# Short-key attention: paired scores on four 32-row groups, and a new order of work per group of eight units

## The reference, cut to what matters

```python
# layer 0, q = layernorm(x), k = v = ctx (77 rows per batch)
qh, kh, vh = (proj(q, Wq, bq), proj(k, Wk, bk), proj(v, Wv, bv))   # 16 heads of 16
scores = einsum('bhqd,bhkd->bhqk', qh, kh) / sqrt(16)
scores = where(mask[:, None] == 0, -1e9, scores)
attn = softmax(scores, axis=-1)
out = einsum('bhqk,bhkd->bhqd', attn, vh) ... @ Wo.T + bo
x = x + tanh(g_xattn[0]) * out

# layer 2, a = the result of the causal self-attention, no mask
c = relu(attention(a, ctx) @ Wo2 + bo2)
c = layernorm(c + c, g2, b2)
f = relu(c @ Wf + bf)
x = x + tanh(g_xattn[2]) * layernorm(c + f, g3, b3)
```

## Time and profile before

| | |
|---|---|
| median of 3 runs | 2646.04 us (2645.72 to 2651.75) |
| the profiled execution's own time | 2645.53 us |
| its span in the profile | 2643.8 us |
| PE matmul busy | 2394.4 us (91%) |
| PE weight loads busy | 1437.0 us (54%) |
| DVE / ACT / POOL busy | 1609.2 / 1298.3 / 1310.7 us (61 / 49 / 50%) |
| `attend_stage`, first scores to the last update | 29.5 to 252.6 us of the span |
| `cross_stage`, first scores to the last update | 1694.6 to 1970.2 us of the span |

### The profile page before, as it was taken

One profiled execution on the slowest core, in us unless ns is written; L12 is line 12 of the kernel. 1 busy time (PEld: TensorE's weight loads), 2 busy tenths in 40 slices (PEclk: granted clock), 3 DMA queues, 4 the chain that ended last, 5 costly groups with the idle time before them and its releaser, 6 DMA issues. The chain is left out here.

```text
span 2643.8 us, 42280 instructions
## 1 busy us (share of the span) xinstructions
PE 2394.4 (91%) x12771; PEld 1437.0 (54%) x12787; DVE 1609.2 (61%) x3275; ACT 1298.3 (49%) x2567; POOL 1310.7 (50%) x2112
## 2 busy tenths in 40 slices
PE   6997999999996986899999999899969966999997
PEld 3554786666663553345444453455546653666664
DVE  5885674655554976777868767598866653221221
ACT  4664454444442883566666666567644421222221
POOL 3665773234445652233443535467865214656663
PEclk9998999999998997999999999999989987999999
DMA  4001000000100005131231311010013151322222
GB/s 142 6 1 54 15 0 1 1 1 1 48 1 16 1 1 128 38 91 37 62 89 33 101 49 49 25 33 17 1 34 135 49 201 29 48 45 44 48 44 28
DMA packets 86128, 115.34 MB, mean 44 GB/s; under 512 B 15480, under 2 KB 65536, under 8 KB 84272
## 3 DMA queue, kind: packets, MB, share of 16 engines
q1 hardware_dynamic: 67408, 92.65, 11.7%
q0 software_dynamic: 18528, 20.31, 4.8%
HBM read 78.01 MB, written 34.64 MB: 43 GB/s over the span
## 5 line engine op out<-in xcount | busy, mean ns | idle before, releaser
L3458 ACT ACTIVATE L2S_pT<-L2S_t_ps 128x512 f32<-128x512 f32 (+3 forms) x768 | 356.5, 491 | 221.6 <-PE L2S_t_ps L3279 213.0
L3522 DVE TENSOR_REDUCE L2S_mx<-L2S_s_ps 128x1 f32<-128x768 f32 (+7 forms) x384 | 350.2, 951 | 104.7 <-PE L2S_s_ps L3202 104.1
L3279 PE MATMUL L2S_t_ps<-L2S_q,L2S_k 98*128 98x512 bf16 (+3 forms) x768 | 249.6, 335 | 17.4 <-DMA L2S_q<-L2S_mrow 7.3
L3764 POOL TENSOR_SCALAR_AFFINE_SELECT L2S_pT<-L2S_pT 128x128 f32<-128x128 f32 x512 | 151.2, 310 | 174.0 <-ACT L2S_pT L3458 169.9
L3201 PE MATMUL L2S_s_ps<-L2S_k,L2S_q 96*128 96x512 bf16 (+3 forms) x768 | 200.0, 333 | 11.5 <-DVE L2S_mx L3522 7.6
L622 POOL TENSOR_TENSOR L_prob<-L_prob,L_rc 128x616 f32<-128x616 f32 x64 | 82.2, 1285 | 231.2 <-DVE L_rc L555 231.2
L4140 DVE TENSOR_TENSOR L3B_h<-L3B_si,L3B_u_ps 128x512 f32<-128x512 f32 x71 | 48.8, 688 | 237.0 <-PE L3B_u_ps L4083 237.0
L4057 POOL DMA_INDIRECT out<-L3B_y,L3F_rows x71 | 114.7, 1616 | 134.5 <-DVE L3B_y L4146 122.3
L3279 PEld LDWEIGHTS L2S_t_ps<-L2S_q,L2S_k 98*128 98x128 bf16 x768 | 73.0, 98 | 197.8 <-ACT L2S_pT L3458 128.4
L3379 PE MATMUL L2S_o_ps<-L2S_pT,L2S_v 128*32 128x512 f32 (+3 forms) x1536 | 166.7, 507 | 0.0
L319 PE MATMUL L_scores<-weights,L_xT 128*128 128x308 f32 x512 | 143.1, 423 | 2.3 <-ACT L_xT L442 1.6
(11 more groups left out here) (548 smaller groups left out, 5748.1 us busy)
## 6 DMA issues: line engine op xcount, KB each, us to landing
qk_parts<-L2S_part SPq DMA_DIRECT2D x84, 128.0 KB, 2.3
L2S_q<-qk_parts SPq DMA_DIRECT2D x32, 192.0 KB, 3.4
L2S_k<-qk_parts SPq DMA_DIRECT2D x30, 192.0 KB, 3.4
L2S_q<-qk_parts SPq DMA_DIRECT2D x32, 128.0 KB, 3.2
L3F_w<-in_L_gu SPq DMA_DIRECT2D x8, 512.0 KB, 7.5
weights<-in_L_w SPq DMA_DIRECT2D x8, 512.0 KB, 9.7
out<-x_sb SPq DMA_DIRECT2D x8, 512.0 KB, 4.0
expert_rows<-L_xn SPq DMA_DIRECT2D x8, 512.0 KB, 3.3
```

Of the source, the lines that this page charges most:

```text
L3279: nc.tensor.matmul(o[:, lo:512], k6[:, q % 2, j, kt * P:(kt + 1) * P], q6[:, q % 2, c, j, lo:512], start=True, stop=True).then_inc(s["t_fu ...
L3458: nc.scalar.activation(pT[:, st % SLOTS, j, lo:512], t_ps[j % 2][:, lo:512], ACT.Exp, scale=SK).then_inc(s["exp_done"], 1)
L3522: nc.vector.tensor_reduce(dst, src, AX.X, ALU.max).then_inc(s["mx_done"], 1)
L3764: nc.gpsimd.affine_select(out=edge, in_=edge, compare_op=ALU.is_ge, fill=0.0, base=0, pattern=[[1, P]], channel_multiplier=-1).then_inc(s[ ...
```

## The change

In both stages:

- `S_ps` is one tile of four banks. `scores(U)` is called for even `U` only and does two units: for each half of the heads (`hf`) four matmuls of 32 rows x 154 columns (two heads of 16 features, 2 x 77 keys), one for each 32-row group `j`, into bank `j`, columns `hf * 154` on. In `attend_stage` four bf16 mask matmuls of 308 columns come first, one for each bank. It waits for `shifted >= U`: both units of the pair before have been subtracted. The start value 2 of `shifted` is gone. DVE reads a unit as 4 banks x 2 heads x 77 where it was 2 banks x 4 heads x 77.
- The step loops and the table are replaced by an order written out per group, one for each engine. The ring's list is rewritten to match.
- In `cross_stage` `stats` of a group, its `rstd` and tile 0 of `scaled` come one group earlier than before, `update` one group earlier, half of the `x` pieces a group earlier, and the program has `G + 4` group steps where it had `G + 5`.

The diff, cut to its core (ACT's order is cut; the pieces keep their bodies):

```diff
-        S_ps = [ctx.enter_context(nc.psum_tensor(f"L0_scores{i}", [P, 2, 512], F32)) for i in range(2)]
+        S_ps = ctx.enter_context(nc.psum_tensor("L0_scores", [P, ROW_GROUPS, 512], F32))   # ROW_GROUPS, WIDE = 4, 2 * NC
...
             def scores(U):                                      # attend_stage, PE
-                pe.wait_ge(shifted, U + 1)
-                for a in range(2):
-                    nc.tensor.matmul(S_ps[U % 2][:, a, 0:BK], identb[:], wide(maskb[...], [P, 4, NC]), start=True, stop=False)
-                for a in range(2):
-                    mm = nc.tensor.matmul(S_ps[U % 2][:, a, 0:BK], qT[64 * a:64 * a + 64, g % 2, hf, i * P:(i + 1) * P],
-                                          kblk[64 * a:64 * a + 64, b % 2, hf, :, :], start=False, stop=True)
-                mm.then_inc(s_full, 1)
+                if U:
+                    pe.wait_ge(shifted, U)
+                for j in range(ROW_GROUPS):
+                    nc.tensor.matmul(S_ps[:, j, 0:2 * WIDE], identb[:], wide(maskb[...], [P, 4, NC]), start=True, stop=False, skip_group_check=True)
+                for hf in range(2):
+                    for j in range(ROW_GROUPS):
+                        mm = nc.tensor.matmul(S_ps[:, j, hf * WIDE:(hf + 1) * WIDE], qT[32 * j:32 * j + 32, g % 2, hf, i * P:(i + 1) * P],
+                                              kblk[32 * j:32 * j + 32, b % 2, hf, 2 * (j % 2):2 * (j % 2) + 2, :],
+                                              start=False, stop=True, skip_group_check=True)
+                mm.then_inc(s_full, 2)
...
             def unit(U):                                        # both stages, DVE
-                s = S_ps[U % 2][:, :, 0:BK].rearrange("p a (h k) -> p a h k", k=NC)
+                s = S_ps[:, :, U % 2 * WIDE:(U % 2 + 1) * WIDE].rearrange("p j (h k) -> p j h k", k=NC)
...
-            dve.sem_inc(shifted, 2)
...
+            # attend_stage, PE, group n (conditions at the ends left out)
+            scores(8n)     turn(8n-3)  turn_x(n+1,0)  values(odd n)  turn_x(n+1,1)  turn(8n-2)  combine(n-2,3)
+            scores(8n+2)   gather(n-1,0)  turn(8n-1)  query(n+1,0)  turn(8n)
+            scores(8n+4)   gather(n-1,1)  turn(8n+1)  query(n+1,1)  turn(8n+2)
+            scores(8n+6)   combine(n-1,0)  turn(8n+3)  combine(n-1,1)  combine(n-1,2)  turn(8n+4)
+            # attend_stage, DVE
+            unit(8n)    unit(8n+1)                                  total(8n)    total(8n+1)
+            unit(8n+2)  unit(8n+3)  stats(n+3,0)                    total(8n+2)  total(8n+3)
+            unit(8n+4)  unit(8n+5)  blocks (odd n) or masks (even)  total(8n+4)  total(8n+5)
+            unit(8n+6)  unit(8n+7)  stats(n+3,1)                    total(8n+6)  total(8n+7)
+            # attend_stage, POOL: the eight divides, with rstd(n+2) and update(n-2,0..3) between, values (odd n)
+            # cross_stage, PE, group g
+            scores(8g)     turn(8g-4)  forward(g-3,1)  turn(8g-3)  forward(g-3,2)  turn(8g-2)  turn_x(g+1,1)
+            scores(8g+2)   turn(8g-1)  forward(g-3,3)  gather(g-1,0)  gather(g-1,1)
+            scores(8g+4)   turn(8g)  combine(g-1,0)  turn_n(g-2,0)  turn(8g+1)  query(g+1,0)  turn(8g+2)
+            scores(8g+6)   turn_n(g-2,1)  combine(g-1,1)  query(g+1,1)  turn(8g+3)  turn_x(g+2,0)  values(odd g)  forward(g-2,0)
+            # cross_stage, DVE
+            unit(8g)    unit(8g+1)  join(g-3,0)  total(8g)
+            unit(8g+2)  total(8g+1)  unit(8g+3)  total(8g+2)  join(g-3,1)  join(g-3,2)
+            unit(8g+4)  total(8g+3)  unit(8g+5)  join(g-3,3)  total(8g+4)  total(8g+5)
+            unit(8g+6)  stats(g-1,0)  unit(8g+7)  stats(g-1,1)  total(8g+6)  blocks (odd g)  total(8g+7)
+            # cross_stage, POOL: the eight divides, with values, scaled(g-2,1..3), update(g-4,1..3), rstd(1,g-3),
+            # rstd(0,g-1) between, and update(g-3,0), scaled(g-1,0) at the end
```

More of the change, by code:

```diff
@@ L1320, in finish_tail @@
                 mm.then_inc(ring_full, 1)
-            piece = {"x": turn_x, "q": query, "o": gather, "c": combine, "n": turn_n, "f": forward, "v": values, "t": turn_tail, "e": finish_tail}
             turn_x(0, 0)
@@ L1576, in _ @@
+            dve.wait_ge(gain_done, 1)
+            for i in range(CH):
+                update(G - 1, i)
         @block.gpsimd
@@ L1649, in _ @@
             pool.wait_ge(gain_done, 1)
-            for s in range(LAST):
-                g, u = divmod(s, UN)
-                if 0 <= s - 2 < UNITS:
-                    divide(s - 2)
-                if (g, u) in ((0, 5), (0, 6)):
-                    bias_tail(u - 5)
-                if (g, u) == (0, 7):
+            for g in range(SPAN):
+                now, old, older, oldest = g < G, 1 <= g <= G, 2 <= g < HERE + 2, 3 <= g <= G + 2
+                if now:
+                    divide(UN * g)
+                if g == 1:
@@ new lines, in _ @@
+                if older:
+                    scaled(g - 2, 1)
+                if now:
+                    divide(UN * g + 1)
+                if older:
+                    scaled(g - 2, 2)
+                if now:
+                    divide(UN * g + 2)
+                if 4 <= g < G + 3:
+                    update(g - 4, 1)
+                if g == 1:
+                    scale_tail(4, 2, 2, 2)
+                if now:
+                    divide(UN * g + 3)
+                if 4 <= g < G + 3:
+                    update(g - 4, 2)
@@ new lines, in _ @@
+                if oldest:
+                    rstd(1, g - 3)
+                if now:
+                    divide(UN * g + 4)
+                if older:
+                    scaled(g - 2, 3)
+                if g == 0:
+                    bias_tail(0)
+                if now:
+                    divide(UN * g + 5)
+                if 4 <= g < G + 3:
+                    update(g - 4, 3)
+                if g == 0:
+                    bias_tail(1)
+                if g == 1:
+                    scale_tail(6, 2, 3, 3).then_inc(tail_done, 1)
@@ L1682, in pipelined @@
+                if old:
+                    rstd(0, g - 1)
+                if now:
+                    divide(UN * g + 6)
+                    divide(UN * g + 7)
+                if 3 <= g < G + 2:
+                    update(g - 3, 0)
+                if 1 <= g < HERE + 1:
+                    scaled(g - 1, 0)
 def pipelined(eng, phases, n=T, unroll=2, ring=2, order=None):
```

605 lines of the change are left out of this document (409 added, 196 removed).

## The result

The changed kernel takes 2625.76 us (median of 4 runs, 2623.97 to 2627.77), the kernel before 2648.62 on the same chip: ratio 0.9914, 95% interval 0.9897 to 0.9931, so 22.9 us faster. The forecast was 2615 with a range of 2594 to 2640. The profiled execution took 2625.5 us, its span is 2623.8.

The account below looks back on a forecast made before the run. PE was taken to bound most groups of both stages, with DVE and POOL close behind after the change. Savings of 14.9 us in `attend_stage` and 16.3 in `cross_stage`, in all 31.2 off 2645.5, gave 2615 us, range 2594 to 2640.

Parts of the forecast that it names:

- Bound and PE's price: Both stages: PE bounds most groups; a pair of scores costs 0.72 us, 1.35 with masks, 3.3 us less per group.
- The rival that the four row tiles don't overlap: Both stages: PE's row tiles don't run side by side, up to 6.6 us a group against the sum, 2676; chance 0.10.
- DVE's terms: Both stages: DVE's reads of scores stay at 1.52 us a unit; bounds 0 and 0.6 us a group.
- The key blocks: DVE in `attend_stage`: key blocks take 1.8 us in a heavy group (every other group, with the value projection).
- rival C: Both stages: orders fit better than walked, groups at the larger sum; attend -20, cross -24, 2601 or below; chance 0.12.
- Forecast 185.5 for eight groups: `attend_stage`: eight groups fall from 199.9 to 185.5 us, -14.4, with heavy groups at 25 and the last at 20.
- the wait for the pair buffer: PE's scores wait until both units of the pair before are subtracted; expected to stay under 1 us a group.
- `cross_stage`, full groups: `cross_stage` groups 3 to 6: from 121.2 to 112 us, 28.0 each, with PE, DVE and POOL all over 0.9 busy.
- Rival D: Both stages: something else paces them, a divide-to-turn chain or the ring; within 5 us of 2646; chance 0.04.
- `cross_stage`, the first three: `cross_stage` groups 0 to 2: from 76.9 to 24 + 26.5 + 23.5 = 74 us, -2.9.
- the first `scaled`: `cross_stage`: POOL's last piece of a group waits for ACT's next `normalise`, divides behind it; within 28.0 per full group.
- `cross_stage`, ends: `cross_stage`: group 7 goes from 24.7 to 26.5 us (+1.8), the end behind the last divide from 46 to 40.

Follow-up runs that it names:

- e2: Changed kernel with the old unpaired scores in two buffers, so the new order alone; 2635.58 us, ratio 0.9947 to the kernel before.
- e8: Changed kernel without the gain multiplication in POOL's residual update of `cross_stage`; 2616.09 us, ratio 0.9868 to the kernel before.
- e11: Changed kernel with POOL's first `scaled` in `cross_stage` moved behind the next group's first divide; 2617.9 us, ratio 0.9883 to the kernel before.
- e4: Changed kernel with ten unread filler matmuls on PE before the second pair in `cross_stage` group 0; 2624.89 us, ratio 0.9901 to the kernel before.

## Why the forecast was right, and where it failed

- **Bound and PE's price.** Right, to 0.01 us a pair. The rival that the four row tiles don't overlap is dead: by the Trainium skill's 3.07 times ("TensorE: Matmul & The Clock Gate", section "Measured speedup vs the span model") the 16 records would have taken an estimated 0.88 us (four rounds at 0.17 and 0.20 of load and drain), and they took 0.73. (One reading of mine was too strong: by my own 0.10 and 0.26 the loads of the earlier trace rows end 0.06 us ahead of the first pass, not long before.) PE fell by more than 3.3 us in a heavy group of `attend_stage`, 27.7 to 23.6, since the order alone took 0.6 of it (27.1 in `e2`).
- **DVE's terms.** The reads of four banks cost nearly what two did: a subtraction 800 ns in both, a maximum on average 772 against 767 in `cross_stage` and 780 against 758 in `attend_stage`, 0.2 us a group. The key blocks were mis-sized: 1.8 us holds a stall, and the two products take 0.47 each now (below).
- **`attend_stage`: mechanism right, size off, rival C nearer.** Forecast 185.5 for eight groups, measured 176.9. Two slips of mine are in the 185.5: I counted three heavy groups where only two take 27.7 us before, and I priced the last window as eight units, where between its first and last divide lie seven (17.3, measured 17.5). Without them my own terms give about 181. Of the other 4 us, the order's saving on PE (0.6 in a heavy group) and the key blocks (0.9) would make 3 in the two heavy groups; the split was not tested. Heavy groups took 23.5 where I had 25, light ones 22.1 to 23.2 against 22 to 23, and the wait for the pair buffer is 6.6 us in seven groups, under 1 us a group as said. The end was forecast 0.5 shorter and is 1.8 longer here, 0.4 in later executions of the same stage; group 0, at 21.9 here, took up to 24.8 in these.
- **`cross_stage`, full groups: near in size.** 113.3 against 112, with POOL busy for 0.86 of it where I had asked for over 0.9. Rival D would have left 121. But pairing had little part in it: the order gives 6.8 of the 7.9 us (by DVE's marks 8.7 of 11.2). The forecast called these groups PE's because PE was busy 116.5 of 121.2; order alone, with the same matmuls, brought PE to 110.8 of 114.3; scores back to back are 16 x 0.20 = 3.2 of these 5.7, the rest I did not trace.
- **`cross_stage`, the first three: the step that failed.** I summed 24 + 26.5 + 23.5 = 74 from DVE's load and got 87.7. Group 0 (30.5) has PE's gap at the start, where the new wait met a DVE that wasn't ready, and the clock behind it; I had looked for that wait in steady groups only, and asked of the clock only that it not fall there (it has 0.97, and 1.00 in `e8` and `e11`). Groups 1 and 2 were to take 50 and take 54.9 by DVE's marks, 27.0 and 27.9. Some 2.5 of it goes with the fallen clock in group 2 (27.9 against 25.4 in `e4`). The rest stays open: `e4` and `e11` still have 53.4 and 53.2, and DVE's load, from which I summed, is 23.9 of 27.0 us in group 1 and 21.3 of 27.9 in group 2, so it alone doesn't set them. POOL's wait for the first `scaled` is not in these groups' time, though POOL's mark for group 1 (31.5) suggests it. The forecast names exactly this wait, as a small part of 28.0 in full groups; it costs some 6 us of the stage, 2.5 in group 5 and 3 behind the start of group 7.
- **`cross_stage`, ends.** Group 7 was to be 26.5, the same slip of seven units for eight; 22.1 measured, -2.6 and not +1.8. The end went from 46.2 to 44.3, not to 40, and what follows took 2.3 us more. POOL's busy time behind the last divide did fall by 7 us, from 34.0 to 26.9, but the final chain got only 1.9 of it: so POOL's queue is not all that sets it. What does was not tested; the 2.3 behind the stage are within the scatter of unchanged stages.
- **The sum.** Forecast -31.2, measured -20.0 between the two spans and -22.9 between medians. It is inside the range because `attend_stage` gave 6 more where `cross_stage` gave 15 less: two misses of opposite sign, which is luck, and the total is a better result than its terms.

## What to carry to other kernels

An added wait for a whole pair is priced by the order around it: the same pairing cost 145 us in the old order and gave time in `attend_stage` in the new one, so look at what the consumer does between the two halves. When an engine's relief gives nothing, look for the in-order queue whose head waits for a later piece, even if that engine is only 86% busy; moving that one call took 6 us or more off a stage that the pairing had made longer. Don't cut groups by the instruction that waits: a late divide made group 1 look 4.5 us longer than DVE's marks show. And walk the first groups of a stage separately: what stands there ahead of the consumer is not in the steady state.

## What the runs showed of the hardware

**Four 32-row tiles overlap.** Sixteen fp32 records of 154 columns take 0.73 us, the same as four records of 64 rows and 308 columns had; their sixteen loads end 0.57 us after the start, inside the matmuls.

**A DVE product of two SBUF operands waits for POOL's divide.** In three of the four pairs of key-block products of `attend_stage` before, the first took 427 to 429 ns and the second 1493 or 1494. DVE's timeline there, then POOL's:

```profile
124.11 1.84 DVE L960 TENSOR_TENSOR L_kblk<-L_kT,headmask_sb 128x308 f32<-128x308 f32 x2
125.87 0.79 DVE L972 TENSOR_REDUCE L_mx<-L_scores 128x8 f32<-128x616 f32 x1
```

```profile
124.27 1.34 POOL L1033 TENSOR_TENSOR L_prob<-L_prob,L_rc 128x616 f32<-128x616 f32 x1 [2.33 <-DVE L_rc L981]
```

The second product starts at 124.46, during POOL's divide, and ends 0.34 us after it (125.95 against 125.61), so it can have done little before POOL was through. In the new order no divide runs there:

```profile
L1020 DVE TENSOR_TENSOR L_kblk<-L_kT,headmask_sb x8: 468/472/478, 17.7 to 162.7; 128x308 f32<-128x308 f32 x8
```

Minimum, median and maximum are within 10 ns. The Trainium skill has this rule ("SBUF — State Buffer", section "SBUF: two separate sides": the pair of ports that both engines use is an exclusive lock for the whole instruction, taken by a DVE operation with two SBUF inputs and by a GpSimd one that reads SBUF); this case agrees, at 1.02 us for each product that starts during a divide. It does not agree for every POOL instruction: POOL's tiny one of 128x4 numbers lasts 1.3 us in `cross_stage` after the change (L1830, from 1733.20), and the product that starts in it, at 1733.55, takes 472 ns.

**The clock fell in and after gaps of PE.** At the start of `cross_stage` PE was idle for 4.8 us, and the same 16 records went from 0.74 to 1.34 us; the level is 1.2 GHz for 17.1 us there. In group 5, behind 3.15 us of waiting, it is 1.2 GHz for 3.4 us and the records take 1.35.
